# Merging the plan of the edge lists into the edge stage of a graph attention kernel

## What is computed

```python
h = jnp.maximum(_layernorm(x, axis=-1), 0.0)
...
h = jnp.einsum('ni,hif->hnf', x, W)
s1 = jnp.einsum('hnf,hf->hn', h, a1)
s2 = jnp.einsum('hnf,hf->hn', h, a2)
scores = jax.nn.leaky_relu(s1[:, :, None] + s2[:, None, :], negative_slope=ALPHA)
scores = jnp.where(adj[None] > 0, scores, NEG_BIG)
att = jax.nn.softmax(scores, axis=-1)
out = jnp.einsum('hnm,hmf->hnf', att, h)
out = jnp.transpose(out, (1, 0, 2)).reshape(N, NHEADS * OUT_FEATS)
return jax.nn.elu(out)
...
x = x + _L0_gnn_ref(h, adj, L0_gnn_W, L0_gnn_a1, L0_gnn_a2)
```

## Time and profile before

| | us |
|---|---|
| median of 3 runs | 788.54 |
| lowest, highest | 784.62, 789.19 |
| the profiled execution | 785.17 |
| its span in the profile | 783.6 |
| outside the span | 1.57 |
| mean granted TensorE clock, share of full | 0.856 |

### The profile page before, as it was taken

The page is one execution under the profiler, slowest core; times in us unless marked ns, Lnnn a source line. Parts: engine busy times, 40 slices in busy tenths (PEclk is TensorE's granted clock), DMA queues, the critical chain, the costliest instruction groups (busy, mean ns, idle before and its releaser), DMA issues.

```text
span 783.6 us, 9125 instructions
## 1 busy us (share of the span) xinstructions
PE 568.1 (73%) x2182; PEld 405.0 (52%) x2182; DVE 650.9 (83%) x1969; ACT 477.8 (61%) x761; POOL 421.9 (54%) x802
## 2 busy tenths in 40 slices
PE   0489789898887777834687656877588659898763
PEld 0245445554444444414566445665466548776652
DVE  4659989999976657954799879999899998999883
ACT  0678887799999979715556546666556314334322
POOL 4634434454333323226767436666747776887860
PEclk9989999999999998965788869777778879998986
DMA  8999999999999999805999999999999887899995
GB/s 279 421 383 396 398 389 379 405 387 420 417 417 419 423 419 423 355 21 190 404 408 415 414 393 321 397 396 401 402 390 374 241 203 188 220 240 289 300 260 162
DMA packets 62395, 269.50 MB, mean 344 GB/s; under 512 B 12050, under 2 KB 12050, under 8 KB 49876
## 3 DMA queue, kind: packets, MB, share of 16 engines
q1 hardware_dynamic: 33524, 185.81, 58.8%
q0 software_dynamic: 25824, 77.31, 32.6%
q10 hardware_dynamic: 2992, 5.77, 2.0%
HBM read 243.49 MB, written 31.13 MB: 350 GB/s over the span
## 4 chain that ended last, share of the span: by engine, by line
DVE 23%; DMA 10%; POOL 9%; issue 9%; ACT 4%; PE 0%; DVEq 0%; POOLq 0%
DVE nodes L1157 9%; DMA nodes<-table,list_column 9%; POOL nodes L990 5%; POOL nodes L985 3%; DVE agg L1169 3%; DVE places L270 2%; ACT result L1049 2%; ACT result L1047 2%; DVE best L259 2%; DVE to_row L1133 1%; DVE result L1177 1%; DMA nodes<-table,column 1%; DVE owner L1098 1%; POOL out_dram L972 1%; PE psC L1288 0%
## 5 line engine op out<-in xcount | busy, mean ns | idle before, releaser
L672 PE MATMUL psH<-sb_W,normedT 128*128 128x512 f32 x384 | 223.0, 672 | 0.0
L249 ACT ACTIVATE packed<-adj_rows,eight 128x3072 uint8<-128x3072 int32 x66 | 188.7, 2858 | 0.8
L985 POOL DMA_INDIRECT nodes<-table,column x138 | 138.0, 1000 | 72.4 <-issue 40.4
L1304 PE MATMUL psP<-nodes,ident 128*128 128x256 f32 x276 | 108.1, 481 | 49.5 <-issue 43.2
L990 POOL DMA_INDIRECT nodes<-table,list_column x109 | 110.0, 1009 | 54.5 <-issue 29.3
L1157 DVE TENSOR_TENSOR nodes<-nodes,psW 128x2048 f32<-128x2048 f32 (+4 forms) x66 | 138.7, 2142 | 0.0
L719 POOL TENSOR_TENSOR sb_node_sum<-sb_node_sum,h_rows 128x512 f32<-128x512 f32 x48 | 61.2, 1274 | 132.2 <-ACT h_rows L637 132.2
L673 PEld LDWEIGHTS psS<-sb_Wa,normedT 128*128 128x128 f32 x384 | 78.1, 203 | 102.1 <-issue 102.1
L270 DVE FIND_INDEX8 places<-best,packed 128x8 uint32<-128x96 f32 (+6 forms) x240 | 110.0, 466 | 0.0
L259 DVE MAX8 best<-packed 128x8 f32<-128x96 f32 (+6 forms) x240 | 102.8, 460 | 4.0 <-ACT packed L249 3.9
L1305 PE MATMUL psP<-nodes,ident 128*128 128x264 f32 x276 | 104.0, 465 | 0.0
(11 more groups left out here) (180 smaller groups left out, 880.1 us busy)
## 6 DMA issues: line engine op xcount, KB each, us to landing
adj_rows<-in_adj_dram SPq DMA_DIRECT2D x66, 1536.0 KB, 10.9
sb_adj_rows<-in_adj_dram SPq DMA_DIRECT2D x30, 1536.0 KB, 14.9
table<-h_rows SPq DMA_DIRECT2D x48, 260.0 KB, 10.0
sb_x_rows<-in_x_dram SPq DMA_DIRECT2D x48, 256.0 KB, 10.3
out_dram<-in_x_dram SPq DMA_DIRECT2D x11, 512.0 KB, 11.8
result<-in_x_dram POOLq DMA_DIRECT2D x11, 512.0 KB, 7.9
out_dram<-result ACTq DMA_DIRECT2D x11, 512.0 KB, 4.9
out_dram<-result POOLq DMA_DIRECT2D x6, 512.0 KB, 6.9
```

The source lines that it names most:

```text
L249: nc.scalar.activation(words.bitcast(mybir.dt.uint8), sb["adj_rows"][buffer_of(i)][:], ACT.Square, bias=sb["eight"][:], scale=-17.0, accum ...
L672: nc.tensor.matmul(psH[:, t % 2], normedT[:, t % 2, kc], sb["W"][:, kc], start=(kc == 0), stop=(kc == KC - 1))
L985: nc.gpsimd.indirect_dma_start(out=nodes[:, node_at[u] + i * w.direct + j], out_offset=None, in_=table, in_offset=bass.IndirectOffsetOnAxi ...
L1304: nc.tensor.matmul(low, sb["ident"][:], nodes[:, n, 0:LOW], start=a, stop=False)
```

## The change

The block of the plan is gone, and its steps are moved.

- **To setup:** the constants of the plan and of the edge stage (`earlier`, `edge_no`, `list_no`, the row numbers in `info`) are made by POOL in the setup block, and the row 0 of the table is stored there from ACT's queue.
- **To stage one:** DVE reduces the s2 of the first 36 tiles in round 37 (`SEEN`), and `count_early` makes the two half counts. PE sums the counts (`psA`, `psB`, now in the bank of `psW`) after its last projection. SP no longer waits for the stores of the table. `node_sum` and `h_rows` take 520 columns instead of 512, so that the mean row has the mean of s2 where it had the bound, and they and other buffers lie in the memory of `nodes`.
- **To the edge stage:** the last addition to `node_sum` (POOL), the range of s2, the bound, places and own scores (DVE and PE), and the mean row, which ACT copies out and stores from its own queue. POOL waits for the stores of the table and of the mean row ahead of its first gather; ACT and PE wait for `placed` ahead of unit 0. The own bounds are written in one step instead of two, for kind A first, and the checks for a fall-back (`check_early`) come after `own(2)`.

The core of the diff:

```diff
+        @block.scalar
+        def _(act):
+            act.wait_ge(no_node_set, 1)
+            act.dma_start(table[0:1], no_node[:]).then_inc(no_node_stored, 16)
+            act.wait_ge(no_node_stored, 16)
...
             sp.dma_start(table[(TILES - 1) * P + 1:N + 1], h_rows[:, (TILES - 1) % HB]).then_inc(stored[(TILES - 1) % HB], 16)
-            for u in range(HB):
-                sp.wait_ge(stored[u], 16 * (TILES // HB))
...
+                if t == SEEN + 1:
+                    dve.wait_ge(h_copied, SEEN)
+                    seen = S2(sb)[:, 0:SEEN].rearrange("p t h -> p h t")
+                    nc.vector.tensor_reduce(sb["most"][:, 0:H], seen, AX.X, ALU.max)
+                    nc.vector.tensor_reduce(sb["most"][:, H:2 * H], seen, AX.X, ALU.min)
...
+            pe.wait_ge(sb["early_listed"], 1)
+            psA, psB = early_sums(sb)
+            nc.tensor.matmul(psA, sb["earlier"][:], sb["listed"][:], start=True, stop=True)
+            nc.tensor.matmul(psB, sb["ones"][:], sb["listed"][:], start=True, stop=True)
...
-            add_up(TILES - 1)
-
-
-def plan(nc, sb, table):
...
         @block.gpsimd
         def _(pool):
-            nc.gpsimd.iota(edge_no[:], [[1, longest * P]], base=0, channel_multiplier=0, allow_small_or_imprecise_dtypes=True).then_inc(made, 1)
-            nc.gpsimd.iota(list_no[:], [[P, longest]], base=0, channel_multiplier=1, allow_small_or_imprecise_dtypes=True).then_inc(made, 1)
+            nc.gpsimd.tensor_tensor(sb["node_sum"], sb["node_sum"], sb["h_rows"][:, (TILES - 1) % HB], ALU.add).then_inc(node_sum_ready, 1)
             nc.gpsimd.memset(rising[:], 0.0).then_inc(late_cleared, 1)
...
+            for u in range(HB):
+                pool.wait_ge(sb["table_stored"][u], 16 * (TILES // HB))
+            pool.wait_ge(mean_stored, 16)
...
-            act.wait_ge(made, 1)
+            act.wait_ge(centred, 1)
             square(0)
             square(1)
+            act.wait_ge(mean_summed, 1)
+            nc.scalar.activation(mean_row[:, 0:HF], ps_mean[0:1], ACT.Copy, scale=1.0 / N).then_inc(mean_made, 1)
+            nc.scalar.activation(mean_row[:, HF:TABLE], ps_mean_s2[0:1], ACT.Copy, scale=1.0 / N).then_inc(mean_made, 1)
+            act.wait_ge(mean_made, 2)
+            act.dma_start(table[N + 1:N + 2], mean_row).then_inc(mean_stored, 16)
             facts_out(0)
...
+            centres()
+            range_of_scores()
+            begins()
+            own_scores("A", 0, 8, 0, 1)
             own(0)
+            extremes()
             own(1)
+            dve.wait_ge(bound_summed, 1)
+            planned(nc.vector.tensor_copy(bound8[:], ps_bound))
+            plan_settles()
+            raise_bound(0, 1)
+            plan_settles()
+            own_bounds("A", 0, 8, 0, 1)
+            plan_settles()
+            dve.sem_inc(placed, 1)
+            raise_bound(1, TILES)
...
+            pe.wait_ge(most_ready, 2)
+            nc.tensor.transpose(ps_most[:, 0:P], most[:, 0:H], sb["ident"][:])
+            nc.tensor.transpose(ps_most[:, P:2 * P], most[:, H:2 * H], sb["ident"][:]).then_inc(most_turned, 1)
+            pe.wait_ge(node_sum_ready, 1)
+            nc.tensor.matmul(ps_mean, sb["ones"][:], sb["node_sum"][:, 0:HF], start=True, stop=True)
+            nc.tensor.matmul(ps_mean_s2, sb["ones"][:], sb["node_sum"][:, HF:TABLE], start=True, stop=True).then_inc(mean_summed, 1)
+            pe.wait_ge(extremes_ready, 2)
+            nc.tensor.matmul(ps_bound, sb["ones"][0:H, :], ext[:], start=True, stop=True).then_inc(bound_summed, 1)
             look_up(0)
```

More of the change, by code:

```diff
@@ L153 @@
 RESTS = max(u.rests for u in UNITS)
+MOST_LISTS = max(u.rest for u in UNITS)
+RING = 36
 def runs(v0, end, what):
@@ L369, in scan_cost, with setup @@
     return 0.3 + 0.00107 * (hi - lo)
-def setup(nc, sb, x, adj, W, a1, a2):
+def setup(nc, sb, x, adj, W, a1, a2, table):
     with ExitStack() as ctx:
@@ L1034, in facts_out @@
                     act.wait_ge(shifted, u - AHEAD + 1)
+                if u == 0:
+                    act.wait_ge(placed, 1)
+                if w.kind != "A" and UNITS[u - 1].kind == "A":
+                    act.wait_ge(placed, 2)
                 s, p0 = w.slots, VISITS[w.parts[0]].place
@@ new lines, in centres, with begins @@
+            def centres():
+                nc.vector.scalar_tensor_tensor(sb["neg_centre"][:, 0:E], psA, -1.0, sb["half_less"][:],
+                                               ALU.mult, ALU.subtract).then_inc(centred, 1)
+            def begins():
+                for kind, v0, v1 in EARLY_KINDS:
+                    s = SLOTS[kind]
+                    planned(nc.vector.tensor_tensor(sb["info" + kind][:, 0:v1 - v0, s:s + 1], psA[:, v0:v1].unsqueeze(2),
+                                                    sb["taken"][:, v0:v1].unsqueeze(2), ALU.subtract))
@@ new lines, in known, with over, raise_bound @@
+            def known(kind, p0, p1, t0, t1):
+                return sb["info" + kind][:, p0:p1, SLOTS[kind] + 2:SLOTS[kind] + 2 + H], sb["info" + kind][:, p0:p1, SLOTS[kind] + 2 + H:SLOTS[kind] + INFO]
+            def over(part, p0, p1, t0, t1):
+                part = part[:, t0:t1]
+                return part if t1 - t0 == p1 - p0 else part.to_broadcast([P, p1 - p0, H])
+            def raise_bound(t0, t1):
+                planned(nc.vector.tensor_tensor(raw[:, t0:t1], S1(sb)[:, t0:t1], bound8[:, 0:H].unsqueeze(1).to_broadcast([P, t1 - t0, H]), ALU.add))
@@ L1245, in _ @@
             own(2)
+            check_early()
             front(1)
@@ L1284, in look_up @@
                     pe.wait_ge(late_planned, 1)
+                if u == 0:
+                    pe.wait_ge(placed, 1)
+                if w.kind != "A" and UNITS[u - 1].kind == "A":
+                    pe.wait_ge(placed, 2)
                 rows = looked(psC, w)
@@ L1545, in build @@
             tmp("earlier", [P, P])
[L1546 removed]
+            tmp("edge_no", [P, MOST_LISTS * P])
+            tmp("list_no", [P, MOST_LISTS])
+            tmp("most", [P, 2 * H])
+            tmp("half_less", [P, EARLY_VISITS])
             tmp("flags", [P, TILES + V + H])
[L1548 removed]
             tmp("column", [P, V, DIRECT], mybir.dt.uint32)
@@ L1572, in build @@
                 sb["x_loaded"] = [scan.enter_context(nc.semaphore(f"x_loaded{u}")) for u in range(XB)]
[L1573 to L1578 removed]
+                sb["degree"] = scan.enter_context(nc.sbuf_tensor("degree", [P, EARLY_VISITS], F32))
+                setup(nc, sb, x, adj, W, a1, a2, table)
                 project_and_scan(nc, sb, x, adj, table, out)
[L1580 removed]
             attend_edges(nc, sb, x, adj, table, out)
```

233 lines of the change are left out of this document (103 added, 130 removed).

## The result

| | before | change |
|---|---|---|
| median, us | 786.91 (4 runs) | 775.81 (4 runs) |
| lowest to highest | 784.62 to 789.19 | 771.59 to 779.86 |
| profiled execution | 785.17 | 777.28 |
| its span | 783.6 | 775.6 |

The ratio to the kernel before is 0.9872, 95% interval 0.9826 to 0.9917. Timed again with more runs it was 0.9860 (0.9817 to 0.9902). The kernel before has one execution more here (785.28) than the three that the prediction knew, whose median was 788.54. The change takes off 11 us of the median, and 8 us between the two profiled executions. Why these two differ is one of the things to settle. Executions over 1.5% above the fastest of the same kernel are left out of the ratios: three of the twelve of `before_seen`, its profiled one among them, and one of the seventeen of the kernel before that were timed beside `sp_waits`, `range_at_once` and `adj_late`.

The account below looks back on a forecast made before the run. A chain of small waiting steps before the full DMA stretch bounds the start; the listed gather moves from 356.57 to 346.6, 10.0 us off 785.17 gives 775.2, off median 788.54 gives 778.5; forecast 777, range 772 to 784.5.

Parts of the forecast that it names:

- What bounds it: Between stage one and the full DMA stretch: a chain of small waiting steps, nothing full; the first listed gather's shift counts.
- The meeting: End of stage one: SP no longer waits for the landing, edge stage opens at 336.2 instead of 338.09, gain 1.9 us.
- The bound, in the new order: Start of edge stage: from 336.2, spreading matmul done at 340.9, placed and look-up 0 at 341.6 instead of 351.54.
- The list: Edge stage, unit 0: listed gather 5.03 us after look-up 0 starts, so at 346.6.
- The table: Mean row landed at 342.7 (at most 1.6 us for issue and landing), direct gathers done 345.6, 1.0 before the list.
- The sum: First listed gather at 346.6 instead of 356.57: 10.0 us earlier, bounds 7.6 to 12.3.
- What is behind it: After the listed gather: first load of adj keeps its 8.2 us distance; the full stretch begins 10 us earlier, DVE's part follows.
- a lost half: Rival, full DMA stretch: half the lead lost as gathers and adj loads share engines; gain 3 to 7, about 780; chance 0.16.
- one more long collision: Rival, edge stage: one more unit waits for a gather behind adj loads; slower, 787, or 791 with four halves; chance 0.05.
- PE stays fast: Rival, edge stage: PE's clock stays up as its idle gap shrinks; gain 12, 772.9; chance 0.10.
- unchanged within 0.5: Sign in the changed kernel's profile: the end of stage one stays where it was within 0.5 us.
- signs of being wrong: Stage one ends later, the mean row lands after 344, or the full stretch grows by what the start won.

Follow-up runs that it names:

- before_seen: Kernel before, with the change's two reductions of 36 tiles of s2 added in round 37 of stage one, result unread; ratio 0.9992 to the kernel before.
- sp_waits: The change, with SP's wait for the landed table stores put back at the end of stage one; ratio 0.9901 to the kernel before.
- range_at_once: The change, with the range of all 48 tiles of s2 taken at once in the edge stage, none in stage one; ratio 0.9895 to the kernel before.
- adj_late: The change, with SP holding the edge stage's first load of adj until unit 0's weights are there; ratio 0.9875 to the kernel before.
- hold_placed: The change, with 13 unread reductions of 384 values more on DVE ahead of the first signal placed; ratio 0.9996 to the kernel before.
- busy_pe_more: The change, with unread matmuls on PE: two 512-wide before the transposes, 256-wide before the bound's and each look-up; ratios 0.9835 and 0.9846 to the kernel before.
- direct_late: The change, with three memsets of 1024 values on POOL between the mean row wait and the first gather; ratio 0.9889 to the kernel before.

## Why the prediction was right

The forecast was a gain of 10.0 us and a time of 777; the measured gains are 11.1 and 11.5, with 10.0 inside both intervals, and the median is 775.81. By its own steps:

- **What bounds it.** The chain through the plan to the first listed gather, with nothing full beside it: shown by `hold_placed`, which restored the time of before by delaying `placed`. That this gather counts and the loads behind the same look-ups do not, `adj_late` bears out for 4.8 us of delay and no further.
- **The meeting, 1.9 us.** Measured from the store's issue to POOL's first instruction 2.52 before and 0.76 after: 1.76, all of it on the path (`sp_waits`).
- **The bound, in the new order.** Forecast 4.7 us from the block's opening to the end of the spreading matmul; measured 341.11 to 345.6, 4.5. `placed` and look-up 0 forecast at 5.4, measured 5.37. The parts were off by more than the sum: DVE's steps until the transposes took 1.4 instead of 1.1 (the section on the hardware has the likely reason), the transposes 0.4 instead of 0.6, the mean sum with its 8 more columns 2.1 instead of 2.4, and the steps from the spreading matmul to look-up 0 0.9 instead of 0.7. That these cancel to 0.03 us is luck.
- **The list.** 4.98 us from look-up to listed gather; forecast 5.03 from the earlier trace rows.
- **The table.** Forecast to be ready 1.0 us before the list. The listed gather's wait for the list is 0.98 us, but 0.30 of it is the gap that stands between one gather and the next in these rows, so 0.7 us were to spare. The step that was mis-sized is the landing: "at most 1.6" us from the store of the mean row to POOL's first gather were 2.12 (345.77 to 347.89). The row that it was read from has an iota behind the wait and not a gather; a memset in the gather's place began after 1.26 us (`direct_late`). It stayed within the 1.0 us that the prediction allowed.
- **The sum.** From store to listed gather 9.9 us less, forecast 10.0.
- **What is behind it.** The distance to the first load of adj is 8.18 us in both kernels, as said, and listed to end took 424.0 to 427.0 before and 423.9 and 424.2 in the change. For a while the lead was smaller: DVE's first score stood 12.3 to 13.0 us behind the listed gather before and 14.3 and 15.4 in the change. At the end no part of it was given back. The rivals of a lost half and of one more long collision have no support in any profile.
- **PE stays fast** did not happen in the change's two profiles (look-ups of 2.8 us). Where it was forced (`busy_pe_more`) it gave 1.5 us and not the 2.3 that the prediction priced, since POOL's path through the mean row then came last.

One sign that the prediction named was wrong: stage one's end "unchanged within 0.5". It was 4.8 later in the first profile of the change, though nothing here shows that the change moves it, and with it every absolute time that the prediction named was some 5 us late: the opening of the edge stage 341.1 for 336.2, look-up 0 346.5 for 341.6, the mean row landed after 344. Two of the three signs of being wrong were thus met by the letter (stage one ends later, the mean row lands after 344). Single executions differ there by up to 8 us (332.3 to 340.3), so an absolute time behind it is no test; a distance between two events on one chain is. The same spread is what made the profiled pair show 8 us where the medians show 11.

## What to carry to other kernels

Between two stages that fill a resource there can be a chain of tiny steps in which nothing is full; here its length came off the total one for one within the 3 us or so that the runs can tell, and the bytes behind it did not shorten the benefit. Find the one event that starts the next full stretch, and measure every edit as the distance to it from the last event of the stage before. Work moved out of such a chain is worth what it takes from that distance. Ask of each stream that starts earlier whether it had to: here the direct gathers gave nothing by themselves (`hold_placed`) and had to be out of the way only before the list was ready, 4.8 us on the loads of adj cost nothing that could be seen, and what waited for `placed` could not be late at all.

## What the runs showed of the hardware

**DVE and POOL hold each other.** In the change two DVE instructions are stretched exactly to the end of a POOL addition with two inputs:

```profile
336.07 1.28 POOL L749 TENSOR_TENSOR nodes<-nodes 128x520 f32<-128x520 f32 x1 [5.14 <-ACT nodes L663]
336.17 1.22 DVE L477 COPY nodes<-degree 128x28 f32<-128x28 f32 x1
341.82 0.59 DVE L1031 TENSOR_TENSOR most<-most,most_late 128x8 f32<-128x8 f32 x1
342.33 0.15 DVE L1032 TENSOR_TENSOR most<-most,most_late 128x8 f32<-128x8 f32 x1
```

The copy of 28 values ends at 337.39, the addition at 337.35; the addition of 8 values ends at 342.41, POOL's at 342.39, and its twin right behind takes 0.15. By this some 0.4 us of the path to the bound are a wait that no semaphore shows (an estimate from 0.59 and 0.15): the moved addition costs DVE, where the prediction had only looked at POOL being held. It is no wait of every DVE instruction: two reductions of 96 values ran beside the same addition in 0.31 and 0.32 us. The Trainium skill, Advanced Engine Details and Errata, section Mode Summary, says that GpSimd and 2-port Vector instructions block each other; the copy's row agrees (1.22 us, where the timeline of before has 0.17 for the same copy). `range_at_once`, whose reductions need one input, has no such wait and lost only 0.35 us by reducing 384 values twice where the change reduces 96.

**TensorE's clock fell at different places of the same chain.** With the same instructions the sum for the mean row took 1.91 us in the change, 1.02 in `direct_late` and 1.37 in `adj_late`, and all three had their look-ups at 2.8. PE had been without matmuls for 2.5 us ahead of the transposes in each. The granted clock reached 0.50 in that gap in the change, behind the start of the sum in `adj_late` (1.00 from 339 to 340 us, 0.53 from 340 to 341, the sum at 339.52), and behind its end in `direct_late` (0.83 from 338 to 339, the sum from 336.82 to 337.84). In `busy_pe_more`, where PE was busy for 4.96 of the 5 us from 335 to 340, it stayed at 1.00, which is 2.4 GHz, through the first look-up.
